# One copy of the last layer's buffers, and its closing work placed among the tiles of the next quarter

## The reference, cut to what matters

```python
h = h + _L1_attn_ref(_layernorm(h))     # positional phase memory, then a norm and a product with out_w
h = h + _L1_ffn_ref(_layernorm(h))      # router, softmax, top 2 of 6 experts, three products each

def _L1_ffn_ref(features, router_w1, router_b1, ...):
    rh = jax.nn.relu(features @ router_w1 + router_b1)
    expert_logits = jax.nn.softmax(rh @ router_w2 + router_b2, axis=-1)
    top_w, top_i = jax.lax.top_k(expert_logits, TOP_K)
    routing_weights = jax.nn.softmax(top_w, axis=-1)
    h1 = relu(einsum('bsd,edh->bseh', features, expert_w1) + expert_b1)
    h2 = relu(einsum('bseh,ehf->bsef', h1, expert_w2) + expert_b2)
    expert_out = einsum('bsef,efo->bseo', h2, expert_w3) + expert_b3
    ...                                  # weighed sum of the two chosen
```

## Time and profile before

| | |
|---|---|
| median of 3 runs | 1347.37 us (1346.24 to 1347.96) |
| the profiled execution's own time | 1345.62 us |
| its span in the profile | 1343.6 us |
| busy in the span | PE 91%, DVE 58%, ACT 48%, POOL 39% |
| first tile of the last layer on PE | 1010.3 us |
| first quarter's tiles end, 2nd, 3rd begin on PE | 1061.1, 1117.4, 1174.2 us |
| last tile's `masked` on PE | 1218.7 us |

### The profile page before, as it was taken

How to read it: one execution, slowest core, us unless ns; L and a number is a source line. 1 busy time by engine, 2 the same in 40 slices (tenths; PEclk the granted TensorE clock), 3 DMA queues, 4 the chain that set the end, 5 groups by cost and what they waited for, 6 DMA issues and landing times.

```text
span 1343.6 us, 27026 instructions
## 1 busy us (share of the span) xinstructions
PE 1228.2 (91%) x10203; PEld 785.8 (58%) x10203; DVE 780.1 (58%) x1724; ACT 641.1 (48%) x1372; POOL 526.5 (39%) x1110
## 2 busy tenths in 40 slices
PE   6889999999999999999999998699718888889998
PEld 5755565665666666666666665455415676676553
DVE  3545555665556566566566562142677898984542
ACT  1325555555554554554545544050245754744564
POOL 3211454754554644555455444405880120421200
PEclk8969999999999999999999999699858677568999
DMA  4100000000000000000000001012110000000001
GB/s 84 18 5 2 2 3 2 4 6 2 3 3 2 3 3 2 2 2 2 3 2 3 2 3 33 5 75 61 18 16 0 1 1 0 13 1 1 13 12 23
DMA packets 34076, 14.57 MB, mean 11 GB/s; under 512 B 30738, under 2 KB 31346, under 8 KB 33949
## 3 DMA queue, kind: packets, MB, share of 16 engines
q1 hardware_dynamic: 29341, 10.95, 3.6%
q0 software_dynamic: 4608, 1.91, 1.6%
HBM read 6.46 MB, written 7.27 MB: 10 GB/s over the span
## 4 chain that ended last, share of the span: by engine, by line
PE 73%; DVE 11%; POOL 5%; issue 5%; ACT 4%; SPq 2%; DMA 1%; POOLq 0%; DVEq 0%; ACTq 0%
PE psum L755 21%; PE psum L736 10%; PE psum L664 8%; PE psum L727 8%; PE psum L711 4%; POOL XN L1310 3%; PE psum L1008 2%; PE psum L649 2%; DVE arena L1978 2%; PE psum L558 2%; PE psum L988 1%; PE psum L669 1%; PE psum L809 1%; PE psum L822 1%; PE psum L1023 1%
## 5 line engine op out<-in xcount | busy, mean ns | idle before, releaser
L1428 ACT ACTIVATE arena<-psum 125x500 f32<-125x500 f32 x576 | 306.9, 585 | 337.7 <-PE psum L736 337.7
L1779 DVE TENSOR_REDUCE arena<-psum 125x1 f32<-125x500 f32 x384 | 242.4, 673 | 201.7 <-PE psum L664 201.7
L664 PE MATMUL psum<-arena 32*125 32x500 f32 (+1 forms) x1536 | 323.3, 517 | 0.6 <-ACT arena L1419 0.6
L755 PE MATMUL psum<-arena,XN 125*64 125x250 f32 x2304 | 307.9, 388 | 0.2 <-ACT arena L1428 0.2
L736 PE MATMUL psum<-arena 32*125 32x250 f32 x2304 | 291.7, 370 | 0.0
L736 PEld LDWEIGHTS psum<-arena 32*125 32x125 f32 x2304 | 214.6, 183 | 11.8 <-issue 1.0
L755 PEld LDWEIGHTS psum<-arena,XN 125*64 125x64 f32 x2304 | 140.3, 136 | 121.3 <-issue 78.6
L1782 DVE TENSOR_REDUCE arena<-psum 125x2 f32<-125x500 f32 x192 | 121.2, 673 | 71.7 <-PE psum L664 67.5
L664 PEld LDWEIGHTS psum<-arena 32*125 32x125 f32 x1536 | 126.8, 183 | 4.2 <-ACT arena L1419 1.2
L727 PE MATMUL psum<-arena,onesb 3*125 3x500 bf16 x576 | 122.4, 422 | 1.4 <-DMA arena<-arena 1.4
L1204 POOL TENSOR_TENSOR lnst<-lnst,mhalf 125x12 f32<-125x12 f32 x14 | 32.0, 2286 | 227.6 <-DVE lnst L1758 227.6
(11 more groups left out here) (342 smaller groups left out, 1970.9 us busy)
## 6 DMA issues: line engine op xcount, KB each, us to landing
arena<-arena SPq DMA_DIRECT2D x192, 1.5 KB
expert_in<-XN SPq DMA_DIRECT2D x8, 256.0 KB, 4.8
arena<-expert_in SPq DMA_DIRECT2D x4, 512.0 KB, 4.9
expert_out<-arena SPq DMA_DIRECT2D x4, 512.0 KB, 2.8
out<-H SPq DMA_DIRECT2D x16, 93.8 KB
expert_in<-XN,slot_in POOLq DMA_INDIRECT x48
XN<-expert_out,slot_out POOLq DMA_INDIRECT x48, 3.3
arena<-in_L_ffn_w SPq DMA_DIRECT2D x2, 256.0 KB
```

What stands on the lines that cost most here:

```text
L664: last = pe.matmul(ps[0:R, at_:at_ + hi - lo], QH[row:row + 32, b, g, j * R:(j + 1) * R], KH[row:row + 32, b, g, lo:hi], start=True, stop= ...
L755: last = pe.matmul(ctx_bank[64 * h2:64 * h2 + 64, 0:THIRD], XN[:, p, c, a, :], PR[:, x % 4, h2, i * THIRD:(i + 1) * THIRD], start=(c == 0) ...
L1428: act.activation(PR[:, x % 4, h2, :], st_bank[(2 * x + h2) % 3][0:R, 0:2 * THIRD], ACT.Exp)\
L1779: dve.reduce_max(MX[:, q % 2, 0, 2 * h2 + tile:2 * h2 + tile + 1], ps[0:R, 0:2 * THIRD], AX)\
```

## The change

Features are kept for two quarters in place of three (`p % 2` for `p % 3`), and of HG, KG, SG, CX, RH, GP, YS there is one copy, of H2 six halves for twelve. That leaves room for the expert buffers beside the features. The experts' weights go to `qkp` and `vox`, which layer 0's attention has left, so POOL's clearing no longer waits for a place: it stands before the event loop. The closing work of each quarter follows a rule, two events to a tile, one behind `features` and one at the tile's end: twelve events in six tiles, for quarter p from x = 6p + 8. Steps start at x = 14. Within a step `layer3` and `summed` now come first. Waits are added where the single copies are written again.

```diff
-        ROOM, FIRST, PER = 16, 23, 1
-        norm_at = {0: (8, 9, 10, 11, 12, 13, 14, 16), 1: (14, 15, 16, 17, 18, 19, 20, 22),
...
-        gate_at = {0: 19, 1: 23, 2: 29, 3: 35}
+        FIRST = 14
+        chain = [("centre", 2), ("variance", 2), ("normalize", 2), ("transpose", 2), ("product", 0), ("centre", 3),
+                 ("variance", 3), ("transpose", 3), ("router",), ("logit",), ("weighed",), ("gates",)]
+
+        def late(x, slot):
+
+            return [(*chain[n], p) for p in range(NP) for n in (2 * (x - NJ * p - 8) + slot,) if 0 <= n < len(chain)]
...
             if x < NT:
                 events.append(("features", x))
+            events += late(x, 0)
...
-            if x == ROOM:
-                events.append(("room", 0))
-            for _ in range(PER if x >= FIRST else 0):
-                k = todo[0][1]
-                if x > gate_at[steps1[min(k, len(steps1) - 1)][0]] + 3:
-                    events.append(todo.pop(0))
+            events += late(x, 1)
+            if x >= FIRST and todo:
+                events.append(todo.pop(0))
...
                 elif kind == "step":
+                    if x >= 4 and x % 3 == 1:
+                        layer3(x // 3 - 1)
                     if x < len(steps1):
                         layer1(x)
                     if 1 <= x <= len(steps1):
                         gate_spread(x - 1)
                         layer2(x - 1)
-                    if x >= 4 and x % 3 == 1:
-                        layer3(x // 3 - 1)
...
             gather(3)
 
+            pool.memset(b3r, 0.0)
+            pool.memset(e2w, 0.0).then_inc(S["late_zero"], 1)
+            link(pool.memset(GP, 0.0))
+            for n in range(4):
+                link(pool.iota(out=ramp[32 * n:32 * n + 32, :], pattern=[[1, 6]], base=0,
+                                 channel_multiplier=-1, allow_small_or_imprecise_dtypes=True))
+            pool.tensor_scalar(SEL.rearrange("r p e d -> r (p e) d"), over(ramp, 6, D), 0.0, None,
+                               ALU.is_equal).then_inc(S["select"], 1)
+
             for event in events:
...
             def tokens_out(p, h):
+                if p >= 2 and h == 0:
+                    k = jobs[("ret", NJ * (p - 1) - 1)]
+                    dve.wait_ge(full[k % 8], k // 8 + 1)
...
-                    if n >= 2:
-                        i = jobs[("l3", n - 2)]
+                    if n >= 1:
+                        i = jobs[("l3", n - 1)]
```

More of the change, by code:

```diff
@@ L292, in held @@
         def held(p):
-            return slice(NJ * (p % 3), NJ * (p % 3) + NJ)
+            return slice(NJ * (p % 2), NJ * (p % 2) + NJ)
         def held2(p):
-            return slice(2 * NJ * (p % 3), 2 * NJ * (p % 3) + 2 * NJ)
+            return slice(2 * NJ * (p % 2), 2 * NJ * (p % 2) + 2 * NJ)
         def phases_of(p, heads, keys):
@@ L356, in build @@
                                ("normalize", 1, p + 2), ("transpose", 1, p + 2), ("mean", p + 2)][k])
-            for p in range(NP):
-                for n, name in enumerate((("centre", 2), ("variance", 2), ("normalize", 2), ("transpose", 2),
-                                          ("product", 0), ("centre", 3), ("variance", 3), ("transpose", 3))):
-                    if norm_at[p][n] == x:
-                        events.append((*name, p))
-            for p in range(NP):
-                if 0 <= x - gate_at[p] <= 3:
-                    events.append((("router", "logit", "weighed", "gates")[x - gate_at[p]], p))
-            if x == ROOM:
-                events.append(("room", 0))
-            for _ in range(PER if x >= FIRST else 0):
-                k = todo[0][1]
-                if x > gate_at[steps1[min(k, len(steps1) - 1)][0]] + 3:
-                    events.append(todo.pop(0))
+            events += late(x, 1)
+            if x >= FIRST and todo:
+                events.append(todo.pop(0))
         events += todo
@@ L851, in hidden @@
                     cols = slice(p * L + th * HALF, p * L + (th + 1) * HALF)
-                    own = slice(p % 2 * L + th * HALF, p % 2 * L + (th + 1) * HALF)
+                    own = slice(th * HALF, (th + 1) * HALF)
                     for name, w in (("hop", W["hop1"]), ("sg", W["sg1"])):
@@ L869, in tokens @@
                     cols = slice(i * R, (i + 1) * R)
-                    own = slice((i - p // 2 * 2 * NJ) * R, (i - p // 2 * 2 * NJ + 1) * R)
+                    own = slice((i - NJ * p) * R, (i - NJ * p + 1) * R)
                     ps, done = take(pe, ("tok", i))
@@ L898, in masked @@
                 p, j = divmod(x, NJ)
[L899 removed]
+                g = 2 * NJ * (p % 2) + 2 * j
                 for k in range(2):
@@ L1336, in _ @@
                     scale(x, event[2])
-                elif kind == "room":
-                    k = jobs[("ao", NT - 1)]
-                    pool.wait_ge(full[k % 8], k // 8 + 1)
-                    pool.memset(b3r, 0.0)
-                    pool.memset(e2w, 0.0).then_inc(S["late_zero"], 1)
-                    link(pool.memset(GP, 0.0))
-                    for n in range(4):
-                        link(pool.iota(out=ramp[32 * n:32 * n + 32, :], pattern=[[1, 6]], base=0,
-                                         channel_multiplier=-1, allow_small_or_imprecise_dtypes=True))
-                    pool.tensor_scalar(SEL.rearrange("r p e d -> r (p e) d"), over(ramp, 6, D), 0.0, None,
-                                       ALU.is_equal).then_inc(S["select"], 1)
         @block.scalar
@@ L1493, in hidden @@
             def hidden(p):
+                if p:
+                    k = jobs[("ao", NJ * p - 1)]
+                    act.wait_ge(full[k % 8], k // 8 + 1)
                 for th in range(2):
-                    own = slice(p % 2 * L + th * HALF, p % 2 * L + (th + 1) * HALF)
+                    own = slice(th * HALF, (th + 1) * HALF)
                     emptied(act, ("hop", p, th))
@@ L1532, in memory_features @@
                 p, c = divmod(q, 3)
-                g = slice(2 * NJ * (p % 3) + 4 * c, 2 * NJ * (p % 3) + 4 * c + 4)
-                tiles = slice(NJ * (p % 3) + 2 * c, NJ * (p % 3) + 2 * c + 2)
+                g = slice(2 * NJ * (p % 2) + 4 * c, 2 * NJ * (p % 2) + 4 * c + 4)
+                tiles = slice(NJ * (p % 2) + 2 * c, NJ * (p % 2) + 2 * c + 2)
                 act.wait_ge(S["rg"], p + 1)
@@ L1667, in _ @@
                 elif kind == "step":
+                    if x >= 4 and x % 3 == 1:
+                        summed(x // 3 - 1)
                     if x < len(steps1):
@@ L1671, in _ @@
                         hidden2(x - 1)
-                    if x >= 4 and x % 3 == 1:
-                        summed(x // 3 - 1)
         @block.vector
```

117 lines of the change are left out of this document (55 added, 62 removed).

## The result

The changed kernel takes 1396.83 us (median of 4 runs, 1395.41 to 1397.15) against 1347.30 (4 runs, 1346.24 to 1347.96): ratio 1.0362, 95% interval 1.0346 to 1.0377. It is slower, as forecast, by 49.5 us and not by 20.4, and it lies above the range (1340 to 1388).

The account below looks back on a forecast made before the run. DVE was taken to set the pace in tiles 6 to 17, PE behind the last tile. 3.5 + 4.3 + 14 + 16.2 - 17.6 = +20.4 us on 1347.4 gave 1368, own range 1357 to 1376, overall 1340 to 1388.

Parts of the forecast that it names:

- The clearing: Ahead of the first tile: POOL's clearing now stands before work that ACT and PE wait for, uncovered; +3.5 us.
- The lower bound of 2.4: POOL's clearing ahead of the first tile: nearer 2.4 us if DVE is idle when it ends; the sum 1 us lower.
- Tiles 6 to 11, +4.3: Quarter 0's product, centre 3 and variance 3 move here as DVE work that nothing hides; +4.3 us.
- Tiles 12 to 17, +14: New choices, route and two `gated` add 8.2 us on DVE; steps 1 and 2 add 5.8 on PE; +14 us.
- Quarter 0's norm leaves, quarter 1's comes: no change: In tiles 12 to 17, one quarter's norm replaces another's; no change in time.
- Tiles 18 to 23, +16.2: PE's work 47 us at full clock plus 13.7 of stalls: 60.7 against 44.5 us.
- Behind the last tile, -17.6: Work leaving gives -36.4, quarter 1's gates -5, new stalls +21.1, `layer3` +2.9; kept as -17.6 us.
- layer3 first, +2.9: Behind the last tile, `layer3` first in its step waits for the `gated` a step used to cover; +2.9 us.
- Single copies, nothing: Added waits for HG, CX, KG, GP, H2 name results PE finished a quarter or half earlier; no cost.
- steps fit into PE's spare time among the tiles: Overlap rival: steps fill PE's half-clocked time, needing steps 1 to 9 under 10 us; 1338 us, chance 0.21.
- The clock rival: PE's clock halves after stalls, 1.7 us lost after one; +35 us in all, 1382 us, chance 0.22.

Follow-up runs that it names:

- Norms dense: One each, but each quarter's norms and product in four tiles, one event ahead of the chunk, one at the tile's end: 1387.1 us, ratio 1.0294.
- one each: Changed kernel's memory with one closing event a tile, at the tile's end, steps from tile 21, layer3 last in its step: 1356.1 us, 1.0049 of the kernel before.
- steps at 17: Changed kernel with steps starting at tile 17 and not 14: 1404.0 us, 1.0419 of the kernel before.
- gates dense: One each, but router, logit, weighed and gates in two tiles instead of four, steps from tile 18 instead of 21: 1376.6 us, ratio 1.0219.
- Kept busy less: Changed kernel with idle matmuls on PE, only as long as the waits, before quarter 3's transposes and the gates of quarters 2 and 3: 1389.5 us.
- old order: Changed kernel's memory with the order of before: closing work, steps from tile 23, layer3 last in its step, clearing at tile 16: 1352.7 us, ratio 1.0049.
- eight tiles: Changed kernel with a quarter's twelve closing events over eight tiles, not six, and steps from tile 16: 1389.0 us, 1.0314 of the kernel before.
- no power: Changed kernel without POOL's power in the closing norms, so the output differs: 1392.4 us, 1.0337 of the kernel before.

## Why the prediction was wrong

**The sign and the general mechanism** stood: order, not memory, costs (44 of 49.5 us), the tail gives back less than the middle takes, and the waits behind the last tile came as summed: transposes 6.58 and 8.71 (6.5 twice), gates 2.64 and 3.90 (2.8 and 4.1), the last layer3s 1.44; in tiles 18 to 23 the bank of the mask 6.18 (6.2), the transposes 3.46 (4.2), gates 1.07 (2).

**The clearing**: +3.5 in the first tile, measured 4.4 with a last gather that ended 0.9 later. Right in the profile, not confirmed at the end. The lower bound of 2.4 rested on DVE being idle when the block ends; it was in a chunk, and with DVE idle the comparison takes 1.20 and not a few tenths.

**Tiles 6 to 11, +4.3, is the first step that failed.** I charged DVE's added work alone. I had worked out the length of a norm's link (9.4 us) for the end and used it in tiles 21 and 23, but not in tiles 9 and 11, where quarter 0's transposes stand one event or less behind their variance. They waited 3.96 and 7.27, and PE's tokens 5.42 where they had waited 3.66 before: a mask that holds their bank is behind centre 2 and the chunk, the wait that I had priced in tile 20 only. DVE's added work was there, 5.3 us busy for my 4.3, but PE's idle time rose by 14.3. Norms dense against one each gives 13.8 with no more PE work.

**Tiles 12 to 17, +14, is the second: right size by wrong terms.** "Quarter 0's norm leaves, quarter 1's comes: no change" was false, because quarter 1's norm comes with half the spacing: 9.9 us (norms dense against one each). I also counted the steps wrongly: they are 0 to 3, with three `layer2`, not steps 1 and 2. Three of them cost 5.6 in the end (steps at 17), what I had charged for two, because part of them lay inside the wait of tile 17's transposes. Adding 9.9 + 1.7 (one each against before) + 5.6 leaves 2.3 of the 19.5 for choices and route, where I had 8.2; this remainder isn't measured by itself, and without dense norms beside them the dense gates, with the work that came in with them, cost 12.0 there (gates dense), so the split depends on what stands next to it.

**Tiles 18 to 23, +16.2**: PE's work was taken at full clock, 47; it was busy 55.6 at 0.87. The stalls came to 11.4 of idle time instead of 13.7.

**Behind the last tile, -17.6, measured -8.1.** The stalls are nearly right and their length isn't all they cost. The clock term, 1.7 a stall, I had left to a rival with 0.22: my sum left PE 77.6 us of work (114.0 - 36.4), and it was busy 84.9. Kept busy less gives 7.4 back. PE's idle time was summed to 29.9 and came to 31.9: the second transposes waited 2.2 longer and the logit 0.5 shorter, and two readings of the old idle time were off. I struck 5 us for quarter 1's gates, which waited 2.82, and left in quarter 2's 1.39, which the new wait replaces:

```profile
1233.79 1.29 PE L976 MATMUL psum<-ident,arena 125*128 125x125 f32 x6 [2.82 <-DVE arena L2065]
```

**layer3 first, +2.9**: 7.2 on the change, 10.2 on the old order. **Single copies, nothing**: 5.4 on the old order. I said that the waits name results finished long before; H2's names the `layer3` of the same step, and DVE waited for it seven times.

**The rivals.** That steps fit into PE's spare time among the tiles was half right: they cost 5.6 for 13.5 us of PE work. It didn't decide, since the norms cost 24 there. Its condition, steps 1 to 9 under 10 us among the tiles, wasn't measured by itself. The clock rival named the right mechanism and gave 1382; with the norms' links in tiles 6 to 17 (13.8 + 9.9 against 4.3 charged) it would have been some 1401.

**Open**: eight tiles and no power lose most of what their waits free among the tiles. The rows name the instructions that then wait; what each costs in time wasn't taken apart.

## What to carry to other kernels

Work out once how long one link of a chain over several engines takes (here 9.4 us, summed from rows of the tail, from PE's result through DVE, ACT, DVE and POOL back to PE), and lay it against what stands between the two ends in every place, short tiles above all (5.4 us), not only where the profile already shows waits. Where PE sets the pace, as behind the last tile here, a wait costs its length and the half clock behind it. To price a reorder, count what each stretch holds by the kernel's own list, row by row; a stretch in which one block leaves and another comes is unchanged only if the spacing is too.
